# An opening reordered around the indirect gathers, with four subtractions of W_r moved from VectorE to GpSimd

## The reference

```python
h = rmsnorm(layernorm(x), g_res) @ W_in.T + b_in
s = scan(rmsnorm(ctx, g_init)[..., :512])        # s[i] = a * s[i-1] + u[i], over rows
x = x + s[plug] + h                              # plug: patch number of each row
y = layernorm(x)
prev = shift(y, one row)
xr = mu_r * y + (1 - mu_r) * prev
xk = mu_k * y + (1 - mu_k) * prev
x = x + sigmoid(xr @ W_r.T) * (square(relu(xk @ W_k.T)) @ W_v.T)
```

## Time and profile before

| | us |
|---|---|
| median of three runs | 763.05 |
| the profiled execution, whole | 765.53 |
| its span | 764.0 |
| TensorE busy in the span | 742.8 |
| VectorE busy | 586.8 |
| ScalarE busy | 406.7 |
| GpSimd busy | 172.8 |

### The profile page before, as it was taken

One profiled execution on the slowest core, in us unless ns is written; L12 is line 12 of the kernel. 1 busy time (PEld: TensorE's weight loads), 2 busy tenths in 40 slices (PEclk: granted clock), 3 DMA queues, 4 the chain that ended last, 5 costly groups with the idle time before them and its releaser, 6 DMA issues.

```text
span 764.0 us, 11067 instructions
## 1 busy us (share of the span) xinstructions
PE 742.8 (97%) x3432; PEld 614.5 (80%) x3433; DVE 586.8 (77%) x1063; ACT 406.7 (53%) x666; POOL 172.8 (23%) x163
## 2 busy tenths in 40 slices
PE   7968899999999999999999999999999999999998
PEld 4746688888888888888888888888888888888887
DVE  7687897886968768696876969778597877867462
ACT  4347465554537546454754645565463655544860
POOL 6433131313111131311213131131312113130000
PEclk9999999999999999999999999999999999999999
DMA  8747173646437163542716346272633616341011
GB/s 302 211 138 185 63 187 128 156 147 149 146 91 208 55 156 133 138 162 83 219 53 152 136 106 183 67 213 79 158 127 102 199 64 159 131 121 18 1 55 56
DMA packets 51453, 100.02 MB, mean 131 GB/s; under 512 B 5134, under 2 KB 5390, under 8 KB 51388
## 3 DMA queue, kind: packets, MB, share of 16 engines
q1 hardware_dynamic: 41900, 82.46, 31.1%
q0 software_dynamic: 9216, 16.78, 13.8%
q10 hardware_dynamic: 288, 0.27, 0.1%
HBM read 64.26 MB, written 21.76 MB: 113 GB/s over the span
## 4 chain that ended last, share of the span: by engine, by line
PE 90%; DVE 5%; DMA 2%; issue 1%; ACT 1%; POOL 0%; DVEq 0%; POOLq 0%; ACTq 0%
PE bank L561 29%; PE bank L563 28%; PE bank L562 28%; PE bank L697 4%; DMA ring<-s_rows,patch_now 1%; DMA ring<-s_rows,patch_of 1%; PE bank L791 1%; DVE bn_a L1030 1%; DVE bn_b L1173 0%; DVE ring L1168 0%; DVE xt_lo L1001 0%; DVE wi_lo L1001 0%; DVE scratch L1134 0%; POOL ring L505 0%; DVE gate L1388 0%
## 5 line engine op out<-in xcount | busy, mean ns | idle before, releaser
L505 POOL DMA_INDIRECT ring<-s_rows,patch_now x60 | 99.0, 1651 | 226.2 <-DMA s_rows<-scanned 195.5
L1134 DVE SCALAR_TENSOR_TENSOR scratch<-turned,cols,scratch 128x512 f32<-128x512 f32 x128 | 94.6, 750 | 32.7 <-ACT scratch L862 24.3
L1001 DVE TENSOR_TENSOR xr_lo<-scratch,xr_hi 128x512 fp32r<-128x512 f32 x124 | 85.1, 689 | 38.5 <-ACT xr_hi L813 37.5
L813 ACT ACTIVATE turned<-bank 128x512 f32<-128x512 f32 x64 | 33.3, 604 | 138.2 <-PE bank L697 138.2
L561 PE MATMUL bank<-xk_hi,wk_hi 128*128 128x512 f32 x256 | 100.2, 391 | 2.9 <-DVE ring L1168 2.9
L561 PE MATMUL bank<-wi_hi,xt_hi 128*128 128x512 f32 x256 | 101.3, 396 | 0.0
L563 PE MATMUL bank<-xk_hi,wk_lo 128*128 128x512 f32 x256 | 100.3, 392 | 0.0
L562 PE MATMUL bank<-xk_lo,wk_hi 128*128 128x512 f32 x256 | 100.3, 392 | 0.0
L561 PE MATMUL bank<-wr_hi,xr_hi 128*128 128x512 f32 x256 | 99.7, 389 | 0.2 <-issue 0.2
L562 PE MATMUL bank<-wi_lo,xt_hi 128*128 128x512 f32 x256 | 99.7, 389 | 0.0
L563 PE MATMUL bank<-wi_hi,xt_lo 128*128 128x512 f32 x256 | 99.7, 389 | 0.0
(11 more groups left out here) (148 smaller groups left out, 1267.6 us busy)
## 6 DMA issues: line engine op xcount, KB each, us to landing
ring<-in_x SPq DMA_DIRECT2D x16, 1024.0 KB, 5.3
out<-gate SPq DMA_DIRECT2D x63, 256.0 KB
xt<-in_x_turned SPq DMA_DIRECT2D x14, 1024.0 KB, 7.2
above<-scanned SPq DMA_DIRECT2D x42, 224.0 KB, 2.7
ctx_rows<-in_ctx SPq DMA_DIRECT2D x15, 512.0 KB, 6.3
s_rows<-scanned SPq DMA_DIRECT2D x15, 256.0 KB, 2.4
above<-u SPq DMA_DIRECT2D x14, 224.0 KB, 2.6
gate<-in_L_xattn_W_in SPq DMA_DIRECT2D x4, 256.0 KB, 3.5
```

Of the source, the lines that this page charges most:

```text
L505: pool.indirect_dma_start(ring[b.slot][:, t, :], None, s_rows[:, :], bass.IndirectOffsetOnAxis(ap=rows, axis=0), compute_op=ALU.add).then_ ...
L813: return nc.scalar.activation(to, of, ACT.Copy)
L1001: return nc.vector.tensor_tensor(to, whole, high, ALU.subtract)
L1134: nc.vector.scalar_tensor_tensor(scratch[:, 2 + i % 2, :], turned[:, c, 1:S + 1], cols[:, 1 + which, c:c + 1], scratch[:, i % 2, :], ALU.m ...
```

## The change

SyncE issues `load_x` of batch 1 and, behind it, the context of batch 1 only once the first scan's store has landed; W_r behind the landing of batch 0's gathers, in front of W_k; the context of batch 2 behind the landing of batch 1's gathers, where it was behind the scan's store. GpSimd makes the four low parts of W_r, behind `root_b(0)` and ahead of `root_a(1)`; VectorE no longer does. ScalarE rounds part 0 of W_r ahead of `turned_out(0)` and parts 1 to 3 one at a time behind `mix_hi` 0 to 2. TensorE makes all four products of the last projection tile of batch 1 ahead of the transposes of batch 0, behind a wait for two `add_x` of batch 0. VectorE runs `mix_next` 3 ahead of `mix_low` 2, and in the first iteration `ka_low` 0 ahead of the clear, `ka_low` 1 between the statistics of tiles 1 and 2.

```diff
@@ SyncE, opening
             load_part(xt_of(Batch(0, 1)), x_turned[1], 0, C, xt_next_loaded)
+
+            reached(sp, s_stored, Batch(0, 0), 16, 16)
             load_x(Batch(0, 1))
             sp.wait_ge(marks_counted, 1)
             reached(sp, ms_c_done, Batch(0, 0), 1, 1)
             load_ctx(Batch(0, 1))
 
-            reached(sp, s_stored, Batch(0, 0), 16, 16)
+            rows_added(sp, Batch(0, 0))
             reached(sp, xt_lo_ready, Batch(0, 0), 2, 2)
             load_w(WR, w_r)
-
-            rows_added(sp, Batch(0, 0))
             reached(sp, xt_lo_ready, Batch(0, 1), 2, 2)
             load_w(WK, w_k)
@@
             store_scan(Batch(0, 1))
-            reached(sp, s_stored, Batch(0, 1), 16, 16)
+            rows_added(sp, Batch(0, 1))
             reached(sp, far_over, Batch(0, 1), 1, 1)
             load_ctx(Batch(0, 2))
@@ GpSimd, root_b, first batch
+                    for c in range(C):
+                        pool.wait_ge(w_hi_ready[WR], c + 1)
+                        nc.gpsimd.tensor_tensor(wt_lo[WR][:, c, :], staged[WR][:, c, :], f32(wt_hi[WR][:, c, :]),
+                                                ALU.subtract).then_inc(w_lo_ready[WR], 1)
@@ TensorE, first_steps
-                for c in range(C // 2):
+
+                reached(pe, x2_ready, b.plus(-1), T, T - 2)
+                for c in range(C):
                     project_tile(b, T - 1, c)
                 pe.wait_ge(ident_ready, 2)
                 turn(b.plus(-1))
-                for c in range(C // 2, C):
-                    project_tile(b, T - 1, c)
@@ ScalarE, mix_hi and iteration
+                    if is_first(b) and i < C - 1:
+                        weight_hi(WR, i + 1, i + 2)
@@
-                    weight_hi(WR)
+                    weight_hi(WR, 0, 1)
                     turned_out(nxt)
@@ VectorE, iteration(-1)
                     scan_input(new)
-                    weight_lo(WR, 0, 1)
                     stats_a(new, T)
-                    weight_lo(WR, 1, 2)
@@
                     mix_next(nxt, 2)
-                    weight_lo(WR, 2, 3)
+                    mix_next(nxt, 3)
                     mix_low(nxt, 2)
-                    mix_next(nxt, 3)
-                    weight_lo(WR, 3, 4)
@@ VectorE, iteration(0)
                     scan_input(new)
+                    ka_low(b, 0)
                     clear_head(new)
-                    stats_b(nxt)
-                    ka_low(b, 0)
+                    statistics_b(nxt, 0)
+                    statistics_b(nxt, 1)
                     ka_low(b, 1)
+                    stats_b(nxt, 2)
```

## The result

| | before | after |
|---|---|---|
| median, us (runs) | 763.1 (7) | 766.34 (7) |
| range of the runs | 762.49 to 764.76 | 765.47 to 768.72 |
| profiled execution, whole | 765.53 | 766.17 |
| its span | 764.0 | 764.6 |
| transposes of batch 1 start | 91.87 | 92.22 |

The ratio of after to before is 1.003, with a 95% interval of 1.0017 to 1.0044: **slower by 0.3%, 1.3 to 3.4 us**. The quotient of the two medians is larger, 3.2 us, near the upper end of that interval; the ratio's middle is 2.3 us. The forecast was 764.2, 1.1 us slower. Measured is 2.1 us more by the medians and 1.2 by the ratio, within the range. Rival 2 had 766.2, but its landmark, 95.1, is not what the profile shows.

A forecast was written before the change was run, and what follows sets the result against it. TensorE, busy 97% of the span, was taken as the bound, its few waits all early. The front's 3.5 us gain was gone by the value product; 1.2 us of clock loss gave 764.2, range 761.0 to 767.0.

The forecast's parts named there:

- Rival 2: Opening: the port shared with VectorE makes GpSimd the bound; gathers, context and batch 1 transposes 2.0 later; 766.2; chance 0.24.
- landmark: Start of batch 1's transposes, 91.87 us before; the kernel was said to gain or lose what this moment moves.
- The sign and the path: Whole opening: slower, through W_r, GpSimd's fourth subtraction, batch 1's gathers, batch 2's context and VectorE's low parts.
- My sum: First 92 us: front's gain gone by the value product, clock loss 1.2 us; 764.2 us; chance 0.46.
- the difference is carried over to the median: Final conversion: the profiled execution's 2.5 us above before's median 763.05 was kept, giving 764.2 for the change.
- The store: First scan's store, batch 0: lands in 2.0 us instead of 7.1, 5.1 us earlier for what follows.
- The front's gain: Up to batch 0's turned tiles: ready at 44.4, 3.5 us earlier, not 5.1, because W_r is awaited.
- GpSimd, from the turned tiles to the first gather: Rounding, subtraction, root and copy ahead of batch 1's first gather: its issue at 56.0 against 54.99, 1.0 us later.
- The sharing: GpSimd's instructions beside VectorE's with two SBUF inputs: 0.7 us added for GpSimd waiting.
- First gather: Batch 1's first gather: issued at 56.0 us, against 54.99 before.
- From the gathers to the landmark: Key and value products: batch 2's late context enters VectorE's queue; TensorE resumes at 82.0 to 82.3, gain gone.
- The clock: Value product: TensorE waits twice and its clock falls, costing 1.2 us, with 0 and 1.7 as ends.

The follow-up runs named there:

- before_again: The kernel before, unedited, run once more: 764.12 us, ratio to before 0.9989.
- store_as_before: The changed kernel with x and context of batch 1 again issued ahead of the wait for the first scan's store: 768.34 us, ratio to before 1.0059.
- before_wv_first: The kernel before with W_v's second half rounded and subtracted ahead of the squares and scale for batch 2: 764.18 us, ratio to before 1.0000.
- ctx2_early: The changed kernel with the context of batch 2 loaded behind the scan's store of batch 1 again: 765.91 us, ratio to before 1.0013.
- low_on_vector: The changed kernel with the four subtractions of W_r back on VectorE: 764.41 us, ratio to before 0.9991.
- root_between: The changed kernel with GpSimd's root for x of batch 1 ahead of the fourth subtraction: 766.66 us, ratio to before 1.0026.
- vec_wr_early: The changed kernel with W_r's subtractions on VectorE and W_r loaded beside batch 0's gathers: 764.94 us, ratio to before 1.0008.
- wr_early: The changed kernel with W_r's load issued ahead of the landing of batch 0's gathers: 769.68 us, ratio to before 1.0058.
- extra_sub: The changed kernel with three more 256-column subtractions on GpSimd behind the four, into an unread buffer: 769.53 us, ratio to before 1.0057.

## Why the prediction was right, and where it was mis-sized

**The sign and the path were right**, the size was short: 1.1 us forecast, 3.2 by the medians, 2.3 by the ratio. **What was mis-sized is where the sum starts from, more than its steps.** My sum put the landmark of after at 93.1 (91.87 + 1.2). Measured is 92.22, and 92.4 for the median: 0.7 to 0.9 earlier than forecast. But I subtracted from the time the 2.5 us by which the profile of before lay above its median ("the difference is carried over to the median"), as if after's median would lie as far below my sum. It did not: the sum had already taken the slow steps of that one execution of before out, the store of 7.1 us and the gather of 8.33, and then took them off once more. The same sum from the rows of before_again (store issued at 20.79 and landed at 26.82, W_k at 40.03, landmark 90.10) gives turned tiles at 44.2 and a landmark of 92.9, 2.8 us slower; an estimate, but near what was measured. So that the forecast time of rival 2 (766.2) comes near 766.34 is luck: its landmark of 95.1 is 2.9 above the measured one, and the same 2.5 us were taken off it. The steps in order:

*The store.* Predicted to land in 2.0 us instead of 7.1: it took 2.0 in after and 2.0 to 3.4 in the other kernels with this order. Right, but the 7.1 was one execution's: in the kernels with the old order it took 6.0 (before_again), 5.7 (store_as_before) and 3.4 (before_wv_first, where it was issued 2 us later).

*The front's gain.* Predicted turned tiles at 44.4, from W_r issued at 36.2 and landed at 41.6. In after: 37.61, 42.9 and 45.59. A part of this belongs to that execution: its granted clock was 0.50 for 10 us from 14 on, in code that isn't changed, and the first scan's store was issued at 22.57 instead of 20.27. But ctx2_early, whose store was issued at 20.13, has its first `carry` at 45.20, and low_on_vector at 43.71. What scatters is, besides the store, the fourth gather: its issue took 1.56 us in some profiles, 2.3 to 2.6 in others, and its landing, with W_r behind it, 5.0 to 5.7. And before_again had its first `carry` at 47.08, not 47.95. The gain is thus 1.5 to 4.2 us at this point, and the hurried store alone is 2.2 as timed. My 3.5 lies within the profiles, towards their high end.

*GpSimd, from the turned tiles to the first gather.* Predicted 11.6 us, measured 12.5 (45.59 to 58.07), and the same 12.5 in ctx2_early and store_as_before. By terms:

| | predicted | measured in after |
|---|---|---|
| turned tiles to the end of the fourth rounding | 7.5 | 8.2 |
| fourth subtraction and what shares its port | 1.1 + 0.7 | 1.3 |
| root | 1.3 | 1.5 |
| copy and the gap to the gather | 1.0 | 1.5 |

The subtraction was mis-sized by 0.2 to 0.4 us each (1.29 to 1.52 against 1.1, within the ends of 0.5 and 1.7). The estimate from the Trainium skill (GPSIMD Engine Reference, Elementwise — side-by-side cycle accounting), also 1.1, is low by as much. The sharing I had put down as a wait of GpSimd; it came out mostly on the other engine. In after, VectorE:

```profile
43.96 1.76 DVE L1064 SCALAR_TENSOR_TENSOR u<-scratch,rs_c,g_ctx 128x512 f32<-128x512 f32 x1
...
50.85 2.43 DVE L1140 SCALAR_TENSOR_TENSOR scratch<-turned,cols,scratch 128x512 f32<-128x512 f32 x2
```

`u` takes 0.75 us elsewhere and two mixes 1.41. Both started beside a subtraction of GpSimd and grew by 1.0; the two mixes take 2.42 or 2.43 in all seven profiles with the subtractions on GpSimd. I wrote that "the two SBUF inputs of VectorE's mixes can be held up in turn; that is covered". **This step failed as well**: the mixes feed ScalarE's third `mix_hi`, which stands ahead of the fourth rounding, on which GpSimd waits. ScalarE in after shows the wait:

```profile
52.65 0.63 ACT L817 ACTIVATE xr_hi<-scratch 128x512 fp32r<-128x512 f32 x1 [1.42 <-DVE scratch L1140]
53.19 0.62 ACT L817 ACTIVATE wr_hi<-xt 128x512 fp32r<-128x512 f32 x1
```

GpSimd delayed its own input: in low_on_vector this `mix_hi` waits 0.50 us, and the fourth rounding ends 7.3 us behind the turned tiles, not 8.2. The rule of the Trainium skill (SBUF — State Buffer, Who interferes with whom), exclusion for a whole instruction, agrees with these rows in size: 1.0 us more beside subtractions of 1.4 and 1.5.

*First gather.* Predicted 56.0, measured 58.07: 1.2 from the turned tiles, 0.9 from the row of terms above. Rival 2 had its price from gathers 2.0 later and asked for the fourth subtraction to end later than 54: it ended at 55.17, 1.2 of that from the late turned tiles. Its mechanism, GpSimd waiting and 1.7 us long, holds only in half: the length was 1.3, and VectorE did the waiting. And of the 2.1 us at the gather only 0.2 to 0.5 are left at TensorE's last wait, as the next step shows.

*From the gathers to the landmark.* Predicted and measured in after: context's squares done by 72.8, 73.35; W_v subtractions 73.3, 73.91; low parts of the operand done by 76.3, 78.6 and 82, measured 76.93, 79.19 and 82.47; TensorE on at 82.0 to 82.3, 82.52; landmark 93.1, 92.22, since the clock's 1.2 us didn't come. That "VectorE's queue is entered by the context and no longer by the gathers" is shown by ctx2_early, though for some 0.5 to 0.9 us only, since the sums of batch 1 are right behind. That these late numbers are only 0.2 to 0.6 off while the gather is 2.1 off comes in part from landings faster than I put (4.9 and 3.4 us, for 5.2 and 4.2).

*The clock.* I put a fall behind two waits in the value product, 1.2 us. In after it didn't come: the key product ran late, to 79.3, and one wait of 1.70 was left. It fell elsewhere, behind the two waits for the sums. Windows of after, columns as above:

```profile
66.00:68.00 2.00, 1.73 (x4) 1.46 (x5) 1.53 (x4) 2.00 (x5) 0.00 (x0) 0.50 0.77 129
68.00:70.00 2.00, 2.00 (x6) 1.54 (x6) 1.90 (x4) 1.57 (x3) 0.00 (x0) 0.50 0.29 33
70.00:72.00 2.00, 2.00 (x7) 1.54 (x6) 2.00 (x4) 0.00 (x0) 0.00 (x0) 0.50 0.75 265
...
82.00:84.00 2.00, 1.48 (x6) 1.24 (x7) 1.89 (x4) 2.00 (x3) 0.75 (x1) 1.00 0.37 117
```

There it cost nothing that is seen at the last wait, because TensorE ran into VectorE's third low part all the same, and waited 1.70 us for it. Where two waits stood in the value product, the fall came in four kernels and cost 1.6, and didn't come in others (above), so the term was possible, but not due. Over the timed executions the mean granted clock of after is 0.9909 (7) and that of before 0.9932 (89, the three groups). That is a possible share of the 2.3 us, but not all of it: in root_between, which has the subtractions on GpSimd too, the 10 of 12 executions with a clock of 0.991 or more take 766.93 in the mean, and the 24 of 31 such of before beside them 764.52.

*Checks named beforehand.* The store landed by 23: no, by 24.6, with the slow start of that execution. The wait in front of the transposes below 1 us: yes in after, 1.4 in ctx2_early. ScalarE idle until W_r at 41 to 42: 42.9. First gather at 55 to 57: 58. No gather over 6 us: yes. Squares behind 71: yes, 72.2. Two waits in the value product and a fall of the clock: one, and none. Landmark at 92 to 94: yes.

**The sum in timed ratios**, each a difference of two kernels, and so uncertain by some 0.002: the hurried store −0.0029; the subtractions on GpSimd instead of VectorE +0.0039; the late context +0.0017; W_r late instead of early −0.0028. They overlap and don't add up to the whole, but the sign is of use: two parts gained and two lost, though the context's share isn't clear of the noise. The rest of the change (TensorE's products ahead of the transposes, ScalarE's split rounding, `ka_low` and the statistics) was not taken out by itself; all of it is in low_on_vector, at 0.9991.

## What to carry to other kernels

An idle engine is not a free one: ask what stands behind the new work in its queue. Here 2.6 us of subtractions left an engine that carries them without a loss (low_on_vector), and went ahead of the instructions that issue the gathers. Of an instruction on GpSimd that reads beside VectorE, count what it takes from VectorE too, and follow whether this returns to GpSimd as a later input. And where single executions scatter by more than the effect, take the ratio from a dozen of each and use the profile only for the order of events. A sum that starts from one profile starts from that execution's luck as well: here that was 2.5 us, twice the effect forecast.

## What the runs showed that was not expected

- The clock's start varies between executions of the same code: of 14 profiles four have 0.50 for some 10 us from 14 us on (after, wr_early, extra_sub and before_wv_first; vec_wr_early and store_as_before have a shorter stretch), and the first scan's store is issued some 2 us later in these (22.5 to 22.7 for 19.9 to 20.8).
- An indirect gather of 128 rows landed in 4.5 to 5.1 us with no load beside it, 7.2 to 7.6 with 1.5 MB of loads issued just before, and 8.5 to 8.8 with 2.5 MB, at the median of its window; a load "moved earlier" into the gathers took 13.4 us itself (vec_wr_early), for 5.2 alone (low_on_vector).
- The root of 4 columns took 1.02 us alone (low_on_vector) and 1.47 beside a subtraction of VectorE (after); the copy of four columns 0.19 alone and 0.62 beside a mix.
